# Moving three streamed operands of a tuned attention and FFN block to other offsets in SBUF

## The reference

```python
xn = layernorm(x)                                   # without scale and shift
q, k, v = (gelu(xn @ W1 + b1) @ W2 + b2 for each)   # three small MLPs, 256 -> 256 -> 256
scores = (q @ k.T) / sqrt(256 * 512) * tril(ones)   # no softmax
s = layernorm(scores @ v) * ln_w + ln_b
Wq1, Wq2 = ternary(W1), ternary(W2)                 # FFN 256 -> 1024 -> 256
g = silu(relu(xn @ Wq1.T + b1) @ Wq2.T + b2)
out = x + s * g
```

## Time and profile before

| | us |
|---|---|
| median of 3 runs | 307.86 |
| lowest and highest run | 307.18, 310.16 |
| time of the profiled execution | 307.08 |
| its span, first to last instruction | 305.3 |

### The profile page before, as it was taken

One profiled execution on the slowest core, in us unless ns is written; L12 is line 12 of the kernel. 1 busy time (PEld: TensorE's weight loads), 2 busy tenths in 40 slices (PEclk: granted clock), 3 DMA queues, 4 the chain that ended last, 5 costly groups with the idle time before them and its releaser, 6 DMA issues.

```text
span 305.3 us, 5721 instructions
## 1 busy us (share of the span) xinstructions
PE 299.3 (98%) x1852; PEld 268.6 (88%) x1852; DVE 247.9 (81%) x548; ACT 222.2 (73%) x428; POOL 132.8 (43%) x104
## 2 busy tenths in 40 slices
PE   8999999999999999999999999999999999999994
PEld 8878899889988899888997889888998889988893
DVE  4989898957999589975999669995799858696686
ACT  3696958966785957949489577868679594895862
POOL 3954835076060942439151670608515291404100
PEclk9999999999999999999999999999999999999999
DMA  7960044500006000240005100060001500020001
GB/s 236 374 217 1 1 140 137 182 26 0 3 2 206 0 0 0 65 141 0 0 0 145 62 0 0 1 204 2 0 0 39 168 0 0 0 71 2 0 2 69
DMA packets 15228, 19.06 MB, mean 62 GB/s; under 512 B 1776, under 2 KB 12528, under 8 KB 15216
## 3 DMA queue, kind: packets, MB, share of 16 engines
q1 hardware_dynamic: 14656, 18.51, 18.6%
q10 hardware_dynamic: 560, 0.40, 0.4%
HBM read 14.69 MB, written 4.22 MB: 62 GB/s over the span
## 4 chain that ended last, share of the span: by engine, by line
PE 87%; DVE 6%; DMA 3%; SPq 1%; ACT 1%; issue 1%; POOL 0%; DVEq 0%
PE bank L849 86%; DMA x_all<-in_w1t 3%; DVE g L653 1%; SPq L199 1%; DVE gw L767 1%; DVE gw L645 0%; DVE w1q L598 0%; DVE x_all L647 0%; PE bank L957 0%; DVE e L756 0%; PE bank L958 0%; ACT r_lo L402 0%; DVE s_lo L738 0%; DVE gw L796 0%; PE bank L833 0%
## 5 line engine op out<-in xcount | busy, mean ns | idle before, releaser
L743 DVE TENSOR_TENSOR r_lo<-bank,r_hi 128x512 fp32r<-128x512 f32 x64 | 44.0, 691 | 34.7 <-ACT bank L465 34.6
L464 ACT ACTIVATE r_hi<-bank,col 128x512 fp32r<-128x512 f32 x64 | 47.0, 734 | 24.3 <-PE bank L849 24.3
L361 POOL TENSOR_TENSOR o_rstd<-o_var,neg_half 128x2 f32<-128x2 f32 x16 | 11.2, 699 | 82.8 <-ACT o_var L495 82.8
L465 ACT ACTIVATE bank<-bank,col 128x512 f32<-128x512 f32 x64 | 45.4, 710 | 0.0
L320 POOL TENSOR_TENSOR y<-y,xn 128x512 f32<-128x512 f32 x12 | 19.8, 1648 | 55.6 <-DMA y<-in_x_t 55.6
L849 PE MATMUL bank<-xT_lo,w1q 128*128 128x512 f32 x128 | 39.5, 390 | 0.0
L849 PE MATMUL bank<-xT_hi,w1q 128*128 128x512 f32 x128 | 39.5, 390 | 0.0
L443 ACT ACTIVATE g<-bank,col 128x512 fp32r<-128x512 f32 x48 | 34.2, 713 | 1.3 <-PE bank L849 1.1
L849 PE MATMUL bank<-w2q,r_lo 128*128 128x256 f32 x256 | 34.6, 278 | 0.0
L849 PE MATMUL bank<-w2q,r_hi 128*128 128x256 f32 x256 | 34.3, 276 | 0.0
L444 ACT ACTIVATE bank<-bank,col 128x512 f32<-128x512 f32 x48 | 33.0, 688 | 0.0
(11 more groups left out here) (143 smaller groups left out, 684.8 us busy)
## 6 DMA issues: line engine op xcount, KB each, us to landing
out<-x_all SPq DMA_DIRECT2D x15, 256.0 KB, 3.1
x_all<-in_x SPq DMA_DIRECT2D x7, 512.0 KB, 3.6
xn<-x_norm_rows SPq DMA_DIRECT2D x6, 512.0 KB, 4.0
y<-in_x_t SPq DMA_DIRECT2D x6, 512.0 KB, 4.7
x_all<-in_w1t SPq DMA_DIRECT2D x2, 512.0 KB, 7.6
x_all<-in_w2t SPq DMA_DIRECT2D x1, 1024.0 KB, 10.2
row<-in_rows SPq DMA_DIRECT2D x1, 512.0 KB, 4.7
x_all<-in_x SPq DMA_DIRECT2D x1, 256.0 KB, 3.2
```

Of the source, the lines that this page charges most:

```text
L361: nc.gpsimd.tensor_tensor(o_rstd[:, half], o_var[:, half], neg_half[:, half], ALU.pow).then_inc(o_rstd_made, 1)
L464: nc.scalar.activation(r["hi"][:, f], pre[:], ACT.Relu, bias=b1)
L465: nc.scalar.activation(pre[:], pre[:], ACT.Relu, bias=b1).then_inc(f1_whole, 1)
L743: nc.vector.tensor_tensor(r["lo"][:, f], bank[(AT_F1 + f) % BANKS][:], r["hi"][:, f].bitcast(FP32), ALU.subtract).then_inc(r_split, 1)
```

## The change

Three padding tiles are added ahead of three operands, and the scratch tiles behind these are made smaller by as much. `gap_v` (32 bytes) stands ahead of `w2v`, `gap_q` (192 bytes) ahead of `w2q`, and `small` loses 224 bytes (of its 144 columns the kernel uses the first 20; 88 remain). `gap_a` (96 bytes) stands ahead of `v`, and `x_part` loses 96 bytes (of 16 rows 4 are used; 10 remain). Nothing else of the program is touched: the instructions, their order, their shapes and their waits are the same.

```diff
--- before.py
+++ after.py
@@ -68,9 +68,11 @@
         z_bias = sb("z_bias", [P, CK])
         d_weight = sb("d_weight", [P, CK])
         d_const = sb("d_const", [P, 1])
+        gap_v = sb("gap_v", [P, 8])
         w2v = {"hi": sb("w2v_hi", [P, CK, C], FP32R), "lo": sb("w2v_lo", [P, CK, C], FP32R)}
+        gap_q = sb("gap_q", [P, 48])
         w2q = sb("w2q", [P, FT, C], FP32R)
-        small = sb("small", [P, 144])
+        small = sb("small", [P, 88])
         w = {"hi": sb("w_hi", [P, 4, CK, C], FP32R), "lo": sb("w_lo", [P, 4, CK, C], FP32R)}
         w1q = sb("w1q", [P, CK, F], FP32R)
         gap = sb("gap", [P, 112])
@@ -80,12 +82,13 @@
         y = sb("y", [P, TT, C])
         gw = sb("gw", [P, TT, C])
         v32 = sb("v32", [P, TT, C])
+        gap_a = sb("gap_a", [P, 24])
         v = {"hi": sb("v_hi", [P, TT, C], FP32R), "lo": sb("v_lo", [P, TT, C], FP32R)}
         abs_sum = sb("abs_sum", [P, CK + 1])
         thr = sb("thr", [P, 2])
         neg_thr = sb("neg_thr", [P, 2])
         x_stats = sb("x_stats", [P, TT, 6])
-        x_part = sb("x_part", [P, 16, TT])
+        x_part = sb("x_part", [P, 10, TT])
         x_norm = sb("x_norm", [P, 2, TT])
         x_mean, x_rstd = x_norm[:, 0], x_norm[:, 1]
         x_var = sb("x_var", [P, TT])
```

## The result

The changed kernel takes 309.77 us (median of 20 runs, 309.52 to 310.50) against 308.44 before (20 runs, 307.18 to 310.16). The ratio is 1.0042, 95% interval 1.0033 to 1.0051: slower by 0.4%. The profiled execution took 309.75, with a span of 308.0.

The account below looks back on a forecast made before the run. TensorE, busy 98% of the span, was taken as the bound: matmul paces plus a drain. A change of 0 to -0.3 us on the profiled 307.08 or median 307.86 gave 307.5 us, range 306.0 to 310.2.

Parts of the forecast that it names:

- the 309.9 that I gave for FFN two alone: FFN two: only its 512 matmuls go to the slower pace, 4.6 ns each, 2.4 us; one-group cases together 0.10.
- the floor: TensorE matmuls: common lowest start-to-start pace, 113.3 ns for 256 columns and 226.7 for 512, 17/16 of full speed's time.
- the part on the loss: W2v, FFN two, values: loss bounded at 3.4 us (W2v's pace) or 5.8 us (scores' excess) on 752 matmuls; taken as zero.
- most relations seem to settle there: Streamed against loaded starts: 928 against 928 and 352 against 928 run at 113.3 or 226.7 ns, so loss taken as zero.
- a pace of 6.8% above it: Scores stage: 3.63 us for 7,680 columns against 3.40 at the floor, read as a slower pace throughout.
- 5.8 us: The 752 matmuls at the floor: loss if they took the scores' 6.8% excess, giving 313.3 us.
- Rival (a): W2v, FFN two, values: new offsets miss the floor; 752 matmuls cost 3.4 us (310.9) or 5.8 (313.3); full chance 0.14.
- 0.10 in part: Chance that one of the three operand groups alone goes to the slower pace, 308.6 to 309.9 us.
- this wait stays: W2v: at most 0.9 us to win over 8 batches, part of it TensorE's wait on g_lo, which was to remain.
- Rival (b): All 944 matmuls: the 17/16 is a placement cost that multiples of 64 bytes remove, 6.2 us, giving 301.3; chance 0.06.
- Rival (c): The three moved operands: starts are not what the sizes say, so no effect, 307.1 to 307.9 us; chance 0.04.
- The sign that I had set against the relation of two starts: Changed kernel's profile: a stage whose operands did not move changes its pace, which would make the prediction wrong.

Follow-up runs that it names:

- The scans: Programs with none of the reference's arithmetic, only TensorE working: settings of 32 matmuls with streamed or loaded starts stepped; 113.3 to 123.3 ns a matmul at 256 columns.

## Why the prediction was wrong

The time, 309.77, lies within the range, near its upper end, but I forecast no change or a small gain, and the kernel is slower: not only the size was off. That the time lies next to the 309.9 that I gave for FFN two alone is partly luck: FFN two alone does make the ratio 1.0041, but in the change all three operands are off the floor, and two other terms (below) hide more than half of it. The step that failed is in the part on the loss: "I take zero here too", because "most relations seem to settle there". I read the settling at 352 and at 928 as something that most offsets would do. The scans say that at 256 columns the floor was reached at two differences of the eight in steps of 32 bytes: -64, where the kernel stood before, which settles in some settings and stays at 117.8 ns in others, and +64, which settled once. The other six never did, and all three moved operands landed on such places: W2v at -32, FFN two at -96, the values at +32. Stages of 512 columns, which I took as a second case that settles, say nothing of this, since the right difference depends on the width: 0 for 512 columns, where 256 columns take 120.0 ns.

I also misread the scores. Their 0.23 us above the floor looked like a pace of 6.8% above it, but about half stands in their last three matmuls, which stream 512 columns in all and take 0.34 us (109.78 to 110.12) against 0.23 at the floor. One line of the timeline of before:

```profile
109.78 0.34 PE L957 MATMUL bank<-g,z_lo 128*128 128x128 f32 x2
```

In the scan, 128 columns take 111.7 ns wherever they start, and 384 columns 173.3 at best, where the floor would be 170.0. So 5.8 us was never a price of this change.

Rival (a) was the right mechanism, at 0.14 in full and 0.10 in part. Its price of 4.6 ns on 752 matmuls, 3.4 us, measured 2.4 us on the 512 of FFN two and 0.7 on the 240 of values, 3.05 in all (sums over the eight batches of the two traces; 116.7 ns for the values is less than 117.9). Two terms made this into 1.3 at the medians. One, about 0.4 us, is the wait on g_lo, which takes up part of what TensorE loses ahead of it. W2v itself lost nothing, and the kernel with W2v alone moved shows a ratio of 1.0007. I had written that this wait stays; it fell from 2.3 to 0.6 us. The other is that I took the profiled execution of before, in which FFN two and the values are at the floor in every batch, for the kernel. Its 20 runs have a median of 308.44, 1.36 above it. Of the kernels in which FFN two stands at the same difference, four show some of the eight batches at the upper level (one with all three 256 bytes or more further, two with r moved, four with z moved, five with W2v alone moved), and two show none (all three 32 bytes further, the values alone moved). One such batch costs 5.66 + 3.53 - 5.47 - 3.41 = 0.3 us or more, so some four of them would make the 1.36, an estimate. That the median of before is made of executions with a few such batches is an inference; only one execution of before was traced. Why that median lies anywhere from 307.14 to 308.44 in the five groups of runs is open too. The change has hardly any room to vary in this way, since its FFN two is off the floor in every batch.

Rival (b), the 17/16 as a cost of the placement, falls as argued: no start went below 113.3 ns at 256 columns (in steps of 32 bytes, and of 4 from 64 to 128) or 226.7 at 512 (in steps of 32). Rival (c) falls too, since the stages changed as the new starts have it. The rest of the working held in the change: the stages whose operands did not move kept their pace (scores 3.63 us, first FFN product 226.7 ns; only the first layers have 8.21 us for 36 matmuls in most batches, where they had 8.17), the drain stayed short, and W2v stayed within 2.75 to 2.85 us. The sign that I had set against the relation of two starts, a stage that changes its pace though its operands stay, did come, in the kernels with W2v or z alone moved, if only against the one traced execution of before. So the relation decides which levels a stage can have, but something else decides which of them it takes.

On the Trainium skill: "SBUF — State Buffer", section "Who interferes with whom", by which TensorE has two independent read ports and never waits on anyone, made this change worth zero. The measurements decide otherwise: with all other engines idle, the same stream takes between 113.3 and 123.3 ns a matmul by the difference of two starts.

## What to carry to other kernels

Where TensorE is the bound and each matmul loads its own 128 columns, the start of the streamed operand less that of the loaded one is a parameter of the kernel. In fp32r, at 256 columns, it was worth up to 9% of a stage's pace (123.3 against 113.3 ns). It had a period of 256 bytes, and its right value depends on the number of streamed columns. Scan it in a program with nothing else in it, as one run answers for 32 places, and then put each operand there with padding. When a placement has two levels, judge the kernel by many runs, with the kernel that it is compared to beside it, and look at its pace stage by stage, since one profiled execution may show only the better level.

## What the runs showed that I had not expected

- The pace at 256 columns over differences in steps of 32 bytes: -64 has 113.4 or 117.8 ns, +64 the same two, 32 has 116.7, -32 118.3, 96 120.1, 0 120.0, -96 and 128 between 118.4 and 120.0. Four bytes past -64 it is 123.3, four bytes short of it 120.0.
- The level at -64 can be handed to the next stage: the values at 352 stay at 117.7 ns behind an FFN two at -96 in batches 2 to 6, though not in 0 and 1. In the scan it hangs on the number of matmuls in front (9 or 10).
- At the best placement, 256 and 512 columns take 113.3 and 226.7 ns, 17/16 of the time at 2.4 GHz, in every placement tried. 384 columns take 173.3 ns at best and 128 columns 111.7, which is more than 17/16 of theirs.
- Why the two starts should act on each other in this way is open. The runs show on which addresses the pace depends, not what inside the memory makes it so. What sets the level when a stage is entered, and how to force the lower one, is open too.
